# Cross-attention and expert layer: the rotation's two products moved to GpSimd, its bias to ScalarE

## Chip, cores and metric

One core of one Trainium2 chip. The metric is the device time of one execution in microseconds, the median of the runs.

## What is computed

Two layers in a row on x of shape (64, 64, 256): 64 batches, 64 channels, 256 positions. The change lies in the first, cross-attention with 8 heads of 8 channels, in the rotation of q and k. The second, sixteen experts of which each row uses two, and a shared one, comes after it in program order and is untouched.

```python
x = x + xattn(layernorm(x), ctx, ...)
x = x + ffn(layernorm(x), ...)

q = split_heads(_proj(x, Wq, bq));  k = split_heads(_proj(c, Wk, bk))
def _apply_rotary(pos, t):
    half = t.shape[-1] // 2
    rot = jnp.concatenate([-t[..., half:], t[..., :half]], axis=-1)
    return t * jnp.cos(pos) + rot * jnp.sin(pos)
scores = jnp.einsum('bhtc,bhsc->bhts', q, k) / math.sqrt(K_CH)
p_attn = jax.nn.softmax(scores, axis=-1)
```

## The kernel before

The kernel is five written-out instruction streams, one for each engine (`tensor`, `vector`, `scalar`, `gpsimd`, `sync`), that meet only at semaphores. Each stream walks the same `steps` from r = -8 to 72, and inside a step over eight places k = 0 to 7, one for each head. A step handles several batches at different stages at once (`at.has(off)` asks whether batch r + off exists): scores for the maxima of batch r + 2, transposed scores, exponentials and values of batch r, normalisation of batch r - 1, and, at offset 6, the projection and rotation of one operand of a pair of batches: q in even steps, k in odd ones. The order inside each stream is written by hand and no engine skips ahead.

The rotation, step by step (line numbers of the profile):

- TensorE, k = 4: the projection L1420 into `bank_b` (into `bank_a` at r = -5). The channels are ordered so that the two halves of the rotation lie in partitions 0 to 63 and 64 to 127.
- ScalarE, `swap`, L792: at k = 4 and k = 5, each ahead of that k's Exp (L826), one half of the bank is copied to the other half of the partitions, into `turned`.
- VectorE, k = 5, behind the reciprocal L1190 and the product L1197: L1213 makes `rc` = (bank + bias) x cos, L1215 makes `rs` = (turned + bias) x sin, both 128x256 f32, and counts `s_rope`. For r = -6 and -5 VectorE also does the rest (`split`, L972 to L980).
- GpSimd from r = -4: `qk` = rc + rs (L739), its first bf16 part (L742), the rest after it (L744); then `split_maxima` (L703, L706); then the second and third part (L750, L754). SyncE writes the parts to DRAM (L433) and reads them back as the stacked operands `QK` three steps ahead of their use (L440).

`split_maxima` splits the maxima M of batch r + 2, that VectorE's eight reductions L1157 of the step have made, into two bf16 values, Mb. TensorE transposes Mb at k = 2 of the next step (L1462), ahead of that step's L1376 (values of the second half of the heads), and of its projection L1420 at k = 4. ScalarE copies the transpose out (Mt, L860) and SyncE sends it into Q (L555).

`bank_b` is used in turn by the projection, the transposes of the normalised output (L1485, even steps, k = 6), the output projection (L1446), the transposes of normalised rows (L1504, odd steps, k = 7) and the router (L1453). TensorE's `held` waits for its last reader; for L1485 and L1504 that is `s_rope`, VectorE's products.

GpSimd also has, at the head of a step, three tiny operations in even steps (L717 to L721), and in the odd steps r = 19 to 57 two scatters of rows (L693, indirect DMAs) with a memset behind them (L730), in every second of these with an iota ahead (L681). SyncE waits for the memset before it sends Mt. From r = 58 on there is no rotation.

The functions that the change touches:

## Time and profile before

| what | value |
|---|---|
| median of 3 runs | 749.25 us (746.85 to 752.11) |
| span of the profiled execution (no other time of it is recorded) | 758.6 us |
| busy: TensorE, VectorE, ScalarE, GpSimd | 92%, 79%, 68%, 56% |

A page of the profile gives the busy share of each engine, the span in 40 slices, the chain of work that ended last, and the costliest groups of instructions. The trace behind it gives single instructions: start, length, engine, line, what is written from what, and in brackets the idle time of the engine just before and what ended it ("issue" when nothing in the profile does). PE is TensorE, DVE VectorE, ACT ScalarE, POOL GpSimd, SP SyncE; PEclk is the clock granted to TensorE as a share of 2.4 GHz.

### The profile page before, as it was taken

The page shows a single profiled execution, that of the slowest core. Times are in us where ns is not written, and L with a number is a line of the kernel's source. Part 1 is how long each engine was busy: PE and PEld are TensorE (multiplying, and loading weights), DVE is VectorE, ACT ScalarE, POOL GpSimd, SP SyncE. Part 2 cuts the span into 40 slices and gives each one's busy share as a digit, 9 for nine tenths or more (in the row PEclk, how much of TensorE's full clock was granted, in tenths as well). Part 3 has the DMA queues.
Part 4 walks back from the last instruction along what each step waited for, and adds up shares of the span by engine and source line. Part 5 has one row for each costly group of instructions (what it writes and reads, how often), then busy time and mean ns, then how long its engine had stood idle before and what let it go on. Part 6 is the DMA issues. An engine that isn't in the chain of part 4 may idle for free.

```text
span 758.6 us, 19342 instructions
## 1 busy us (share of the span) xinstructions
PE 697.3 (92%) x5941; PEld 482.6 (64%) x5941; DVE 598.5 (79%) x1597; ACT 512.7 (68%) x1211; POOL 426.0 (56%) x755
## 2 busy tenths in 40 slices
PE   2698999999999999999999999999897999999995
PEld 1355565666666666666666666666565978888784
DVE  6888999899899889989998998998645544466666
ACT  4267787888888888888888888887751155554441
POOL 3554656645756667666666566664344025655562
PEclk9999999999999999999999999999999999999998
DMA  5665543444465455544444444444073535678774
GB/s 170 175 174 161 156 124 107 124 134 145 141 176 156 150 164 147 155 131 138 142 143 152 146 121 149 137 140 153 32 225 116 165 92 162 221 244 279 230 236 151
DMA packets 97147, 118.81 MB, mean 157 GB/s; under 512 B 12821, under 2 KB 81304, under 8 KB 97049
## 3 DMA queue, kind: packets, MB, share of 16 engines
q1 hardware_dynamic: 89684, 100.16, 44.0%
q0 software_dynamic: 6864, 16.93, 6.4%
q8 instruction: 53, 0.87, 0.5%
q10 hardware_dynamic: 500, 0.49, 0.3%
q14 instruction: 46, 0.37, 0.2%
HBM read 76.87 MB, written 42.11 MB: 157 GB/s over the span
## 4 chain that ended last, share of the span: by engine, by line
PE 69%; DVE 12%; POOL 8%; issue 7%; DMA 2%; ACT 1%; another core or an unknown queue 0%; SPq 0%; ACTq 0%; DVEq 0%; POOLq 0%
PE bank_o L1376 13%; PE bank_s L1402 11%; PE bank_st L1439 10%; PE bank_st L1559 9%; DVE M L1157 5%; PE bank_s L1577 4%; PE bank_st L1354 4%; PE bank_b L1420 2%; POOL work L739 2%; POOL parts_sb L742 2%; POOL work L744 2%; PE bank_b L1446 2%; PE bank_a L1494 2%; PE bank_b L1485 2%; PE bank_s L1361 2%
## 5 line engine op out<-in xcount | busy, mean ns | idle before, releaser
L1157 DVE TENSOR_REDUCE M<-bank_s 128x2 f32<-128x512 f32 x512 | 339.3, 682 | 49.4 <-PE bank_s L1402 41.5
L826 ACT ACTIVATE Pr<-bank_st 128x512 f32<-128x512 f32 x503 | 292.6, 598 | 64.0 <-PE bank_st L1439 53.3
L1402 PE MATMUL bank_s<-QK 72*128 72x256 bf16 x1024 | 202.0, 280 | 8.8 <-DMA QK<-parts 5.9
L1439 PE MATMUL bank_st<-QK 98*128 98x256 bf16 x1006 | 195.8, 276 | 0.9 <-ACT Pr L826 0.2
L1376 PE MATMUL bank_o<-Pr,wide 128*32 128x256 f32 x2048 | 140.3, 390 | 0.5 <-ACT Pr L826 0.5
L1402 PEld LDWEIGHTS bank_s<-QK 72*128 72x128 bf16 x1024 | 91.0, 99 | 68.8 <-DVE M L1157 30.6
L739 POOL TENSOR_TENSOR work<-work 128x256 f32<-128x256 f32 x62 | 45.0, 725 | 158.5 <-DVE work L1215 158.5
L766 POOL DMA_INDIRECT results<-Pr,ids_out x79 | 78.5, 994 | 80.4 <-issue 45.7
L1439 PEld LDWEIGHTS bank_st<-QK 98*128 98x128 bf16 x1006 | 90.4, 98 | 45.9 <-ACT Pr L826 18.7
L1559 PE MATMUL bank_st<-QK,xn 128*128 x316 | 82.3, 383 | 1.0 <-issue 1.0
L1376 PEld LDWEIGHTS bank_o<-Pr,wide 128*32 128x32 f32 x2048 | 56.3, 110 | 36.0 <-issue 15.0
L693 POOL DMA_INDIRECT slots<-ring,slot x64 | 63.8, 996 | 26.2 <-issue 11.5
L1254 DVE TENSOR_TENSOR OT<-work,bank_st 128x128 f32<-128x128 f32 x79 | 22.7, 288 | 56.9 <-ACT work L917 50.7
L792 ACT ACTIVATE turned<-bank_b 64x256 f32<-64x256 f32 x126 | 47.6, 378 | 19.0 <-PE bank_b L1420 10.4
L1559 PEld LDWEIGHTS bank_st<-QK,xn 128*128 128x128 f32 x316 | 54.0, 190 | 6.7 <-issue 2.2
L1577 PE MATMUL bank_s<-wd,work 128*128 x158 | 47.4, 383 | 0.2 <-DVE Pr L1272 0.2
L742 POOL TENSOR_TENSOR parts_sb<-work 128x256 bf16<-128x256 f32 x62 | 44.9, 724 | 0.0
L754 POOL TENSOR_TENSOR parts_sb<-work,parts_sb 128x256 bf16<-128x256 f32 x62 | 41.7, 673 | 4.9
L865 ACT ACTIVATE O<-bank_o 128x256 f32<-128x256 f32 x64 | 24.5, 383 | 29.4 <-PE bank_o L1376 29.4
L744 POOL TENSOR_TENSOR work<-work,parts_sb 128x256 f32<-128x256 f32 x62 | 41.5, 669 | 4.9
L750 POOL TENSOR_TENSOR parts_sb<-work,parts_sb 128x256 bf16<-128x256 f32 x62 | 41.7, 672 | 0.0
L917 ACT ACTIVATE work<-bank_st 128x128 f32<-128x128 f32 x79 | 21.9, 277 | 27.4 <-PE bank_st L1559 26.3
(175 smaller groups left out, 1061.2 us busy)
## 6 DMA issues: line engine op xcount, KB each, us to landing
QK<-parts SPq DMA_DIRECT2D x127, 288.0 KB
parts<-parts_sb SPq DMA_DIRECT2D x64, 192.0 KB, 2.4
wide<-slots SPq DMA_DIRECT2D x79, 130.0 KB
ctx_kv<-ctx_dram SPq DMA_DIRECT2D x64, 128.0 KB, 2.4
xT_all<-results SPq DMA_DIRECT2D x14, 512.0 KB
QK<-w_gu SPq DMA_DIRECT2D x8, 512.0 KB
parts<-parts_sb SPq DMA_DIRECT2D x31, 128.0 KB, 2.9
X<-x_dram SPq DMA_DIRECT2D x7, 512.0 KB, 5.4
```

Source lines behind the costliest of these rows:

```text
L693: pool.indirect_dma_start(out=slots, out_offset=bass.IndirectOffsetOnAxis(ap=slot[:, k, n:n + 1], axis=0), in_=ring[:, row, :], in_offset= ...
L739: nc.gpsimd.tensor_tensor(qk[:, h], rc[:, h], rs[:, h], ALU.add).then_inc(s_qk, 1)
L742: nc.gpsimd.tensor_tensor(parts[:, p, h, 0, :], rc[:, h], rs[:, h], ALU.add).then_inc(s_p1, 1)
L744: nc.gpsimd.tensor_tensor(rest[:, h], qk[:, h], parts[:, p, h, 0, :], ALU.subtract).then_inc(s_r1, 1)
L766: pool.indirect_dma_start(out=results, out_offset=bass.IndirectOffsetOnAxis(ap=ids_out[:, at.mod(8, -4):at.mod(8, -4) + 1], axis=0), in_=y ...
L826: nc.scalar.activation(Pr[k][:], bank_of_scores(at.r, k)[:], ACT.Exp, scale=SCALE).then_inc(s_exp, 1)
L1157: nc.vector.tensor_reduce(M[:, c, 2 * ORDER[k]:2 * ORDER[k] + 2], bank_s[S_BANK[c][k]][:].rearrange("p (a s) -> p a s", a=2), AX.X, ALU.ma ...
L1376: last = nc.tensor.matmul(bank_o[32 * j:32 * j + 32, 0:T], Vcols[at.odd_pair(off)][:, first:first + 32], Pr[4 * group + j][:, T * chunk:T ...
L1402: last = nc.tensor.matmul(bank_s[S_BANK[at.mod(2)][k]][:, T * t:T * t + T], Q[c][0:KR, ORDER[k], P * t:P * t + P], K[c][0:KR, ORDER[k], :] ...
L1439: last = nc.tensor.matmul(bank_of_scores(at.r, k)[:, T * s:T * s + T], K[c][0:MROW + 2, ORDER[k], P * s:P * s + P], Q[c][0:MROW + 2, ORDER ...
L1559: last = nc.tensor.matmul(up_bank[m][:, 0:2 * I], xTs[m][:, c, :], weights(c), start=(c == 0), stop=(c == 1))
L1577: nc.tensor.matmul(down_bank[m][:, 0:T], aT[m][:, 0:P], weights, start=True, stop=True).then_inc(s_d, 1)
```

## The change

ScalarE adds the biases. Both turned copies become Identity activations with the bias as a pointer (a column of `bias_qk`), and behind the second stands a new one, straight, of the whole bank into a new tile `flat`, counted by a new semaphore `s_flat`. GpSimd makes both products from SBUF: `rs` from `turned` as soon as both copies are there, counted by a new `s_rs`, `rc` from `flat`, counted by `s_rope`. VectorE keeps products only for r = -6 and -5. The readers of `bank_b` that wait for the rotation now wait for `s_flat`. At r = -6 ScalarE waits for the bias before its first copy, since the bias now enters there.

```diff
@@ gpsimd, step
                     p, h = at.odd_pair(6), at.mod(2)
+                    wait(pool, s_turn, at.value(2, 14))
+                    wait(pool, s_p1, at.value(1, 5))
+                    nc.gpsimd.tensor_tensor(rs[:, h], turned[:], tab[:, 1, :], ALU.mult).then_inc(s_rs, 1)
+                    wait(pool, s_flat, at.value(1, 7))
+                    nc.gpsimd.tensor_tensor(rc[:, h], flat[:], tab[:, 0, :], ALU.mult).then_inc(s_rope, 1)
                     wait(pool, s_rope, at.value(1, 7))
+                    wait(pool, s_rs, at.value(1, 7))
@@ scalar, swap
-                wait(act, s_rope, at.value(1, 6))
-                nc.scalar.activation(turned[C * half:C * half + C], bank[C - C * half:P - C * half, 0:T],
-                                     ACT.Copy).then_inc(s_turn, 1)
+                wait(act, s_rs, at.value(1, 6))
+                if at.r == -6:
+                    act.wait_ge(s_bias, 2)
+                own = slice(C * half, C * half + C)
+                h = at.mod(2)
+                nc.scalar.activation(turned[own], bank[C - C * half:P - C * half, 0:T], ACT.Identity,
+                                     bias=bias_qk[own, 2 * h + 1:2 * h + 2]).then_inc(s_turn, 1)
+                if half:
+                    wait(act, s_rope, at.value(1, 6))
+                    nc.scalar.activation(flat[:], bank[:, 0:T], ACT.Identity,
+                                         bias=bias_qk[:, 2 * h:2 * h + 1]).then_inc(s_flat, 1)
@@ vector, step, k == 5
-                        wait(dve, s_turn, at.value(2, 14))
-                        wait(dve, s_p1, at.value(1, 5))
...
-                        bank = bank_a if at.r == -5 else bank_b
-                        nc.vector.scalar_tensor_tensor(rc[:, h, :], bank[:, 0:T], bias_qk[:, 2 * h:2 * h + 1],
-                                                       tab[:, 0, :], ALU.add, ALU.mult)
-                        nc.vector.scalar_tensor_tensor(rs[:, h, :], turned[:], bias_qk[:, 2 * h + 1:2 * h + 2],
-                                                       tab[:, 1, :], ALU.add, ALU.mult).then_inc(s_rope, 1)
+                        if at.r < -4:
+                            wait(dve, s_turn, at.value(2, 14))
+                            wait(dve, s_flat, at.value(1, 7))
+                            nc.vector.tensor_tensor(rc[:, h, :], flat[:], tab[:, 0, :], ALU.mult).then_inc(s_rope, 1)
+                            nc.vector.tensor_tensor(rs[:, h, :], turned[:], tab[:, 1, :], ALU.mult).then_inc(s_rs, 1)
@@ tensor, readers of bank_b (and the two held() calls ahead of L1485 and L1504)
-                return ((s_rope, at.value(1, 6), NB), (s_BTe, at.pairs(last, add=1), NP),
+                return ((s_flat, at.value(1, 6), NB), (s_BTe, at.pairs(last, add=1), NP),
```

How the change moves instructions. GpSimd, a step with an iota and scatters in the steady part, before (`work` is the tile that holds rc, rs, qk and rest):

```order
L681 IOTA ring 128x4
L693 DMA slots<-ring,slot 67712x260 x2
L730 MEMSET stored 1x1
L739 TENSOR_TENSOR work<-work 128x256
L742 TENSOR_TENSOR parts_sb<-work 128x256
L744 TENSOR_TENSOR work<-work,parts_sb 128x256
L703 TENSOR_TENSOR Mb<-M,newton 128x16
L706 TENSOR_TENSOR Mb<-M,Mb 128x16
L750 TENSOR_TENSOR parts_sb<-work,parts_sb 128x256
L754 TENSOR_TENSOR parts_sb<-work,parts_sb 128x256
```

and the same place after:

```order
L684 IOTA ring 128x4
L696 DMA slots<-ring,slot 67712x260 x2
L733 MEMSET stored 1x1
L741 TENSOR_TENSOR work<-turned,tab 128x256
L743 TENSOR_TENSOR work<-flat,tab 128x256
L748 TENSOR_TENSOR work<-work 128x256
L751 TENSOR_TENSOR parts_sb<-work 128x256
L753 TENSOR_TENSOR work<-work,parts_sb 128x256
L706 TENSOR_TENSOR Mb<-M,newton 128x16
L709 TENSOR_TENSOR Mb<-M,Mb 128x16
L759 TENSOR_TENSOR parts_sb<-work,parts_sb 128x256
L763 TENSOR_TENSOR parts_sb<-work,parts_sb 128x256
```

Two instructions of 128x256 now stand between the memset and the sum, and so ahead of the split of the maxima. ScalarE, the rotation of an even step before (`Pr` are the Exps):

```order
L865 ACTIVATE O<-bank_o 128x256
L826 ACTIVATE Pr<-bank_st 128x512
L792 ACTIVATE turned<-bank_b 64x256
L826 ACTIVATE Pr<-bank_st 128x512
L792 ACTIVATE turned<-bank_b 64x256
L826 ACTIVATE Pr<-bank_st 128x512 x2
L847 ACTIVATE ring<-X,vv 128x256
```

and after:

```order
L882 ACTIVATE O<-bank_o 128x256
L843 ACTIVATE Pr<-bank_st 128x512
L805 ACTIVATE turned<-bank_b,bias_qk 64x256
L843 ACTIVATE Pr<-bank_st 128x512
L805 ACTIVATE turned<-bank_b,bias_qk 64x256
L809 ACTIVATE flat<-bank_b,bias_qk 128x256
L843 ACTIVATE Pr<-bank_st 128x512 x2
L864 ACTIVATE ring<-X,vv 128x256
```

The turned copies keep their places; the straight one stands behind the second, ahead of that step's last three Exps.

## Rows read from the trace of the kernel before

**Rows 1.** The page: busy time, share of the span, instructions.

```profile
PE 697.3 (92%) x5941; PEld 482.6 (64%) x5941; DVE 598.5 (79%) x1597; ACT 512.7 (68%) x1211; POOL 426.0 (56%) x755
```

**Rows 2.** The page: the chain that ended last, by line.

```profile
PE bank_o L1376 13%; PE bank_s L1402 11%; PE bank_st L1439 10%; PE bank_st L1559 9%; DVE M L1157 5%; PE bank_s L1577 4%; PE bank_st L1354 4%; PE bank_b L1420 2%; POOL work L739 2%; POOL parts_sb L742 2%; POOL work L744 2%; PE bank_b L1446 2%; PE bank_a L1494 2%; PE bank_b L1485 2%; PE bank_s L1361 2%
```

**Rows 3.** Stretches: length, busy us by engine, clock, DMA share, GB/s.

```profile
76.18:134.82 58.64, 54.98 (x534) 35.12 (x534) 53.88 (x139) 46.52 (x102) 36.16 (x74) 1.00 0.42 126
134.82:511.88 377.06, 365.91 (x3597) 239.22 (x3596) 341.94 (x803) 312.72 (x682) 242.55 (x473) 1.00 0.48 145
```

**Rows 4.** Timeline, one even step: start, length, engine, line, operation, [idle before].

```profile
303.21 0.23 PE L1462 MATMUL bank_a<-ident_b,Mb 128*32 128x128 bf16 x1 [0.19 <-POOL Mb L706]
...
304.90 0.60 PE L1420 MATMUL bank_b<-xn,w_qk 128*128 128x256 f32 x2
...
305.54 0.38 ACT L792 ACTIVATE turned<-bank_b 64x256 f32<-64x256 f32 x1
...
305.94 0.60 ACT L826 ACTIVATE Pr<-bank_st 128x512 f32<-128x512 f32 x1
...
306.56 0.38 ACT L792 ACTIVATE turned<-bank_b 64x256 f32<-64x256 f32 x1
...
307.69 0.48 DVE L1215 SCALAR_TENSOR_TENSOR work<-turned,bias_qk,tab 128x256 f32<-128x256 f32 x1
...
308.24 0.73 POOL L739 TENSOR_TENSOR work<-work 128x256 f32<-128x256 f32 x1 [2.65 <-DVE work L1215]
308.27 0.41 PE L1485 MATMUL bank_b<-ident,On 128*128 128x128 f32 x2 [0.28 <-issue]
...
308.93 0.73 POOL L742 TENSOR_TENSOR parts_sb<-work 128x256 bf16<-128x256 f32 x1
...
309.74 0.67 POOL L744 TENSOR_TENSOR work<-work,parts_sb 128x256 f32<-128x256 f32 x1
...
310.66 0.22 POOL L706 TENSOR_TENSOR Mb<-M,Mb 128x16 bf16<-128x16 f32 x1
...
311.27 0.23 PE L1462 MATMUL bank_a<-ident_b,Mb 128*32 128x128 bf16 x1
```

**Rows 5.** Timeline, the odd steps r = 31 (first row) and r = 33.

```profile
300.52 0.72 POOL L739 TENSOR_TENSOR work<-work 128x256 f32<-128x256 f32 x1 [1.53 <-DVE work L1215]
...
314.63 0.38 ACT L792 ACTIVATE turned<-bank_b 64x256 f32<-64x256 f32 x1
...
314.74 0.09 POOL L730 MEMSET stored<- 1x1 f32 x1
...
316.57 0.72 POOL L739 TENSOR_TENSOR work<-work 128x256 f32<-128x256 f32 x1 [1.74 <-DVE work L1215]
```

**Rows 6.** Groups by line: count, busy us, mean ns of one, idle before, releasers.

```profile
L826 ACT ACTIVATE Pr<-bank_st 128x512 f32<-128x512 f32 x503 | 292.6, 598 | 64.0 <-PE bank_st L1439 53.3
...
L792 ACT ACTIVATE turned<-bank_b 64x256 f32<-64x256 f32 x126 | 47.6, 378 | 19.0 <-PE bank_b L1420 10.4 <-DVE parts_sb L980 3.9
...
L739 POOL TENSOR_TENSOR work<-work 128x256 f32<-128x256 f32 x62 | 45.0, 725 | 158.5 <-DVE work L1215 158.5
...
L865 ACT ACTIVATE O<-bank_o 128x256 f32<-128x256 f32 x64 | 24.5, 383 | 29.4 <-PE bank_o L1376 29.4
...
L837 ACT ACTIVATE xn<-X,shift,rstd 128x256 f32<-128x256 f32 x32 | 19.4, 607 | 0.9 <-DVE shift L953 0.8
...
L853 ACT ACTIVATE ring<-ring 128x512 f32<-128x512 f32 x2 | 1.3, 626 | 0.1
```

**Rows 7.** Timeline, GpSimd and VectorE at the same time.

```profile
303.11 0.67 POOL L750 TENSOR_TENSOR parts_sb<-work,parts_sb 128x256 bf16<-128x256 f32 x1
...
303.20 0.62 DVE L1050 TENSOR_TENSOR CU<-CU,route_sb 128x16 f32<-128x16 f32 x1
...
309.54 0.17 DVE L1050 TENSOR_TENSOR CU<-CU,route_sb 128x16 f32<-128x16 f32 x1
```

**Rows 8.** The chain in order of time, at the start: start, us, what.

```profile
26.45 6.02 DMA parts<-parts_sb
```

More of the change, by code:

```diff
@@ L144, in xattn_moe @@
         turned = sb("turned", [P, T])
+        flat = sb("flat", [P, T])
         beff = sb("beff", [P, 1])
@@ L277, in xattn_moe @@
         s_turn = sem("s_turn")
+        s_rs = sem("s_rs")
+        s_flat = sem("s_flat")
         s_qk = sem("s_qk")
@@ L971, in split @@
                 dve.wait_ge(s_rope, h + 1)
+                dve.wait_ge(s_rs, h + 1)
                 nc.vector.tensor_tensor(qk[:, h], rc[:, h], rs[:, h], ALU.add).then_inc(s_qk, 1)
@@ L1384, in step @@
                 if at.r == -3:
-                    pe.wait_ge(s_rope, 1)
+                    pe.wait_ge(s_flat, 1)
                     nc.tensor.matmul(bank_o[:, 0:1], w[:, 5, :], bias[:, 5:6], start=True, stop=True).then_inc(s_bo, 1)
                 if at.r == -2:
-                    pe.wait_ge(s_rope, 2)
+                    pe.wait_ge(s_flat, 2)
                 if at.r == -1:
@@ L1480, in step @@
                         wait(pe, s_On, at.value(1, 0))
-                        held(at, bank_b, (s_rope, at.value(1, 7), NB))
+                        held(at, bank_b, (s_flat, at.value(1, 7), NB))
                         if at.i is None:
@@ L1499, in step @@
                         wait(pe, s_xs, at.pairs(-5, add=1))
-                        held(at, bank_b, (s_rope, at.value(1, 7), NB))
+                        held(at, bank_b, (s_flat, at.value(1, 7), NB))
                         if at.i is None:
```

## The prediction

> A measurement of this kernel can tell about 1% (7.5 us) from no change; "step" below is one pass r of the main loop, from one transpose of the maxima (L1462 on TensorE) to the next.
>
> **What bounds the kernel now.** I read the busy shares first. TensorE shows 92% and VectorE 79%, GpSimd only 56% [rows 1]. That invites the reading "free VectorE, use GpSimd". The chain of waits corrects it: under TensorE's own lines stand VectorE's reduction L1157 and GpSimd's L739, L742 and L744 [rows 2]. GpSimd is idle for almost half of the time and is on the path all the same.
>
> Next, the stretches. From 134.82 to 511.88 us the clock granted to TensorE is 1.00 (its 2.4 GHz level) and TensorE is busy 365.91 of 377.06 us. Both ends are starts of L1462 and 47 steps lie between, so a step is 8.02 us. The seven steps before (58.64 us) take 8.38 us each, and there VectorE is busy 53.88 us, 92% [rows 3].
>
> Then one step in order of time, the thing to learn here [rows 4]. It starts with L1462 at 303.21, which had waited 0.19 us for GpSimd's Mb. The projection L1420 goes out at 304.90. ScalarE copies the first half turned, 305.54 to 305.92, does one Exp, and copies the second half, 306.56 to 306.94. VectorE's second product ends at 308.17, GpSimd starts its sum L739 at 308.24, goes on with L742 and L744, and only then splits the maxima; L706 ends at 310.88. The next L1462 needs that Mb; it starts at 311.27. The next projection stands behind it in TensorE's order. So there is a ring, TensorE - ScalarE - VectorE - GpSimd - TensorE, that closes once a step. In this even step Mb was 0.39 us early and TensorE was late, for a reason in the same rows: the transpose L1485 into bank b could go only at 308.27, just behind VectorE's products of that bank. In the odd step before it Mb was the late one. Ring and TensorE's own work are nearly equal; what the change does to the ring decides.
>
> **The change, part by part.**
>
> *VectorE loses two instructions a step.* They take 0.47 us each; the second runs from 307.69 to 308.17 [rows 4]. In the ring they are replaced, so nothing is gained there twice. Elsewhere VectorE has room: 341.94 of 377.06 us busy, so I cost this at nothing in the 47 steps; the ring hides it. In the seven early steps at 92% it is worth something: they fall from 8.38 to the ring's new 8.16, -0.22 x 7 = -1.5 us.
>
> *The turned copies get a bias pointer.* ScalarE: a copy from PSUM of 256 elements takes 383 ns and an Exp of 512 takes 598, so an element costs 0.84 ns. A Copy from SBUF of 512 takes 626, so of 256 about 411. The Identity from SBUF of 256, with a pointer for scale and one for bias, takes 607: 196 more, 98 for each pointer [rows 6]. The turned copy of 378 then takes about 0.47. Bounds: 0.38 (the pointer costs nothing) to 0.61 (that Identity's whole time); I take one pointer. Two such copies and one Exp in a row: the second copy ends 0.19 later.
>
> *The straight copy.* 383 + 98 = 0.48 us, behind the second turned copy. It ends at 306.94 + 0.19 + 0.02 + 0.48 = 307.63, before GpSimd wants it (307.89, below). It delays ScalarE's next Exps by 0.67 us together with the rest, but its Exps wait for scores for 53.3 us in the trace, 0.8 us for each of 64 steps [rows 6], and it catches up there. Cost nothing; without that cover up to 0.67 us a step. It also frees bank b at 307.63 instead of 308.17: L1485, which waited 0.28, need not wait. By TensorE's own work an even step would then take 8.06 - 0.28 + 0.09 (scores behind a later Exp) = 7.87 us; an odd one, 2 x 8.02 - 8.06 = 7.98 now, less the 0.19 that L1462 waited, 7.79, and a little less for its own use of bank b: 7.8 on the mean.
>
> *GpSimd gets both products ahead of its sum.* Its sum of two f32 operands takes 725 ns [rows 6]; no product of this size is in the trace. Bounds: 0.67 (L744, one operand bf16) and 0.95 (twice VectorE's 0.47); I take 0.725, same engine, shape and types. Starts in a row stand 0.69 apart where nothing is waited for (308.24, 308.93) and 0.81 where the engine waits for its own result (308.93, 309.74) [rows 4]. So: second turned copy ends 307.13, first product 307.20, second 307.89, sum 308.70, and from the sum's start to Mb's end are 2.64 us as before: 311.34, L1462 at 311.38. The step becomes 311.38 - 303.21 = 8.17, say 8.16 us, odd or even, since no VectorE instruction stands in it any more. TensorE (7.8) now waits for Mb every step. 47 x (8.16 - 8.02) = +6.5 us.
>
> *Steps with scatters.* In 20 odd steps (r = 19 to 57) two indirect DMAs and a memset stand between the tail of one rotation and the head of the next. GpSimd was free at 314.83, idle for 1.74 us, and began the sum at 316.57; the second turned copy had ended at 315.01 [rows 5]. The idleness is now filled by 1.50 us of products. Counted from the step's L1462 at 311.27, GpSimd was free at +3.56. Mb, 0.39 early in the even step ahead, will be just in time, so GpSimd starts its tail 0.35 later and is free at +3.91, and the copy is ready at 3.74 + 0.19 = +3.93: just enough. Ten of the steps have an iota more (idle 1.53 instead of 1.74, as before 300.52 [rows 5]); there the products start some 0.15 late, +1.5 us. The same memset lets SyncE's queue send Mt (L555), now 0.35 to 0.56 us later; TensorE, with 8.16 - 7.8 of new room before L1462, hides most of that.
>
> *The start.* ScalarE now waits for the bias before its first copies. VectorE's first products wait for three copies there. At r = -4 and -3 GpSimd has two rotations in a row, each 1.5 us longer, and behind them goes the write of the parts whose transfer starts at 26.45 in the chain [rows 8]: some 3 us later. The first full steps wait for that data. But the transfer took 6.02 us, among others that would go on meanwhile, so I count +2.5, between 0.5 and 3.5.
>
> Sum: +6.5 + 1.5 - 1.5 + 2.5 = +9.0 us. The profile has a span of 758.6 us (no other time of that execution is recorded), 9.35 above the median of the runs; I put the difference on the median: 749.25 + 9.0 = 758.3.
>
> **A rule against it.** VectorE's L1050 took 0.17 us at 309.54, and 0.62 at 303.20, while GpSimd's L750 ran from 303.11 to 303.78 [rows 7]. The Trainium skill ("SBUF — State Buffer", Who interferes with whom) says that a VectorE instruction with two SBUF inputs and a GpSimd instruction that reads SBUF exclude each other, the later one waiting for the whole of the first. The trace agrees for VectorE as the later one. By that rule 1.45 us more of GpSimd work a step would block VectorE's routing work oftener, which has room, and could hold a product back; for this I have rival D.
>
> **The rivals.**
>
> B, no change: the pointer is read in time that is hidden and the copies stay at 0.38 us. For it: the one ACTIVATE with pointers that I could price reads SBUF, and these read PSUM. Against: both copies begin only at or after the end of what they follow (305.94 + 0.60, then 306.56), so there is nothing under which a read would hide. The ring is then 307.01 + 1.50 + 2.64 + 0.04 = 311.19, 7.98 us; 47 x -0.04 = -2, plus 2.5: 749.8.
>
> C, faster: the ring is not what decides; bank b is. With its wait gone TensorE runs at 7.8 us a step: 47 x -0.22 = -10.3, + 2.5: 741.4. It decides only if Mb is ready by then, which takes both products in under 1.1 us instead of 1.5. Against it stands the 725 ns of 62 sums. The gain of the earlier bank is real and goes into the wait for Mb.
>
> D, still slower: GpSimd cannot keep up in the scatter steps, with blocked products, scatters of 1.0 us behind it and Mt sent late. Twenty steps at 0.4 more: +8, 766. For it: only 0.02 us of room by my count. Against: the remaining wait of TensorE absorbs the Mt part.
>
> E: the copies cost 0.61 each. The ring takes 0.27 more, 8.43: +19 + 2.5, 771.
>
> **How the numbers follow.** Forecast (754 to 763 by itself) 0.53, B 0.20, C 0.06, D 0.15, E 0.06. Slower by over 1% (above 756.7): two thirds of the forecast, D and E, 0.56. Faster by over 1%: C, at 741.4 just past the bound, 0.05. Within 1%: the rest, 0.39. Leaving out C below and E above, the range is 748.5 to 767.
>
> **What would show it.** Right: L1462 starts 8.16 us apart in both kinds of step and every one waits for POOL Mb; the turned copies take 0.47, the straight one 0.48; GpSimd's products 0.725; no wait at L1485; GpSimd's idleness before its first product near 0 in scatter steps and VectorE's share below 85% between the same steps; the parts' write near 29 us. Wrong: steps of 7.98 with copies of 0.38 (B); steps below 7.9 with Mb early (C); odd steps over 8.4 from r = 19 on with GpSimd never idle (D). If TensorE still waits elsewhere (scores, bank s), my claim that ScalarE catches up has failed.

## The result, and the profile after

| | kernel before | changed kernel | ratio, 95% interval |
|---|---|---|---|
| first comparison | 750.68 us (746.85 to 752.31, 4 runs) | 760.22 us (758.41 to 761.23, 4 runs) | 1.0135 [1.0097, 1.0174] |
| second comparison (the experiment "after again") | 748.01 us (745.30 to 750.50, 11 runs) | 758.73 us (755.75 to 761.43, 6 runs) | 1.0142 [1.0114, 1.017] |

The changed kernel is slower by 1.4%, by 9.5 us in the first comparison and 10.7 in the second. The forecast was 9.0 us.

The page of the changed kernel's profile, span 758.7 us, first the busy shares, then the chain that ended last, by engine and by line. TensorE's transpose of the maxima is L1478 now (L1462 before), the projection L1436, the scores L1418, the transposed scores L1455, the turned copies L805, the straight one L809, GpSimd's products L741 and L743, its sum L748, first part L751, rest L753, split of the maxima L706 and L709.

```profile
PE 697.7 (92%) x5941; PEld 482.2 (64%) x5941; DVE 549.7 (72%) x1473; ACT 546.7 (72%) x1275; POOL 515.5 (68%) x879
```

```profile
PE 43%; POOL 33%; issue 8%; ACT 7%; DMA 2%; DVE 2%; POOLq 1%; SPq 0%; ACTq 0%; DVEq 0%
PE bank_st L1575 8%; PE bank_o L1392 8%; PE bank_s L1418 5%; POOL work L748 5%; POOL work L741 5%; POOL parts_sb L751 5%; POOL work L753 5%; POOL work L743 5%; ACT Pr L843 4%; PE bank_s L1593 4%; PE bank_st L1455 4%; PE bank_st L1370 3%; PE bank_b L1436 3%; ACT turned L805 3%; POOL slots L696 2%
```

TensorE's busy share is 92% as in [rows 1], and it tells nothing of what happened. The chain does: GpSimd's lines, 2% of the span each in [rows 2], now stand five times with 5%, and the engine has a third of the chain. VectorE was relieved of 49 us of work (598.5 to 549.7) and the kernel is slower.

The stretches that answer to [rows 3], from one start of L1478 to another: seven early steps, then the 47 steps behind them.

```profile
78.35:135.55 57.20, 54.68 (x534) 35.30 (x534) 48.48 (x124) 49.97 (x109) 45.68 (x88) 1.00 0.43 130
135.55:522.17 386.62, 370.77 (x3596) 239.47 (x3596) 305.80 (x709) 336.44 (x728) 311.24 (x567) 1.00 0.47 141
```

386.62 / 47 = 8.23 us a step, against 8.02: +9.6 us in this stretch alone. The early steps fell from 8.38 to 57.20 / 7 = 8.17, -1.4 us. The clock granted to TensorE is 1.00 in both kernels, so no part of it is a matter of clock.

One even step in order of time, as [rows 4] have it of before. It goes from 291.82 to 300.07.

```profile
291.82 0.23 PE L1478 MATMUL bank_a<-ident_b,Mb 128*32 128x128 bf16 x1 [0.23 <-POOL Mb L709]
...
293.52 0.60 PE L1436 MATMUL bank_b<-xn,w_qk 128*128 128x256 f32 x2
...
294.15 0.47 ACT L805 ACTIVATE turned<-bank_b,bias_qk 64x256 f32<-64x256 f32 x1
...
295.27 0.47 ACT L805 ACTIVATE turned<-bank_b,bias_qk 64x256 f32<-64x256 f32 x1
...
295.77 0.47 ACT L809 ACTIVATE flat<-bank_b,bias_qk 128x256 f32<-128x256 f32 x1
295.82 0.73 POOL L741 TENSOR_TENSOR work<-turned,tab 128x256 f32<-128x256 f32 x1 [1.60 <-ACT turned L805]
296.51 0.81 POOL L743 TENSOR_TENSOR work<-flat,tab 128x256 f32<-128x256 f32 x1
296.51 0.22 DVE L1052 TENSOR_TENSOR route_sb<-route_sb,m 128x64 f32<-128x64 f32 x1
...
296.63 0.44 PE L1501 MATMUL bank_b<-ident,On 128*128 128x128 f32 x2
...
297.39 0.73 POOL L748 TENSOR_TENSOR work<-work 128x256 f32<-128x256 f32 x1
...
299.80 0.22 POOL L709 TENSOR_TENSOR Mb<-M,Mb 128x16 bf16<-128x16 f32 x1
300.07 0.09 PEld L1478 LDWEIGHTS bank_a<-ident_b,Mb 128*32 128x32 bf16 x1 [0.58 <-POOL Mb L709]
300.07 0.23 PE L1478 MATMUL bank_a<-ident_b,Mb 128*32 128x128 bf16 x1 [0.29 <-POOL Mb L709]
```

The reader is to follow GpSimd's column. Once the second turned copy has ended, at 295.74, GpSimd works without a pause until 300.02, the moment at which Mb is there, and TensorE has stood still for it. TensorE's own late one of before, the transpose into bank b (L1485 before, L1501 now), went at +4.81 from the step's start instead of +5.06, as its bank comes free with the straight copy. It gained nothing by that, since the next L1478 waits for Mb. Of the 47 starts of L1478 that end these steps 41 show a wait for Mb, of the load of its weights or of itself (17 before). At the other six, r = 18, 26, ..., 58, TensorE was idle for 0.11 us at most. The list of waits for the stretch has 18.0 us for the loads of weights, in 42 waits (it counts the start at r = 11 too), against 5.0 in 17 before.

Groups by line, the columns as in [rows 6]:

```profile
L805 ACT ACTIVATE turned<-bank_b,bias_qk 64x256 f32<-64x256 f32 x126 | 59.1, 469 | 20.9 <-PE bank_b L1436 10.4 <-DVE parts_sb L998 3.0 <-DVE bias_qk L1226 2.6
...
L743 POOL TENSOR_TENSOR work<-flat,tab 128x256 f32<-128x256 f32 x62 | 45.6, 736 | 0.0
L741 POOL TENSOR_TENSOR work<-turned,tab 128x256 f32<-128x256 f32 x62 | 45.5, 734 | 76.8 <-ACT turned L805 76.0
L748 POOL TENSOR_TENSOR work<-work 128x256 f32<-128x256 f32 x62 | 45.0, 726 | 4.9
...
L809 ACT ACTIVATE flat<-bank_b,bias_qk 128x256 f32<-128x256 f32 x63 | 29.9, 474 | 1.6
```

Last, a step with an iota and two scatters, of GpSimd, SyncE's queue and TensorE. It begins at 300.07 and ends with the last row.

```profile
303.15 0.98 POOL L696 DMA_INDIRECT slots<-ring,slot  x1 [0.30 <-issue]
...
304.12 0.09 POOL L733 MEMSET stored<- 1x1 f32 x1
304.18 0.74 POOL L741 TENSOR_TENSOR work<-turned,tab 128x256 f32<-128x256 f32 x1
304.24 0.68 SPq L558 DMA_DIRECT2D QK<-Mt  x1
...
306.24 0.11 PEld L1455 LDWEIGHTS bank_st<-QK 98*128 98x128 bf16 x2 [0.40 <-DMA QK<-Mt]
...
308.35 0.09 PEld L1478 LDWEIGHTS bank_a<-ident_b,Mb 128*32 128x32 bf16 x1 [0.21 <-POOL Mb L709]
```

GpSimd has no idle time ahead of its first product, which starts at +4.11 instead of +3.99: the scatters hold it. The step takes 8.28. SyncE's load of the scaled maxima, L558, goes only behind the memset, and TensorE waits 0.40 us for it; that wait is hidden here, since L1478 waits again behind it.

### The profile page after: what moved, and what is told of

It reads as the page before. It is cut to its first block, busy times and chain, and to the rows that moved or that the text cites. A ratio compares the mean times of both kernels' runs of the same rounds, so it can differ in the third digit from the quotient of the medians.

```text
span 758.7 us, 19412 instructions
## 1 busy us (share of the span) xinstructions
PE 697.7 (92%) x5941; PEld 482.2 (64%) x5941; DVE 549.7 (72%) x1473; ACT 546.7 (72%) x1275; POOL 515.5 (68%) x879
## 4 chain that ended last, share of the span: by engine, by line
PE 43%; POOL 33%; issue 8%; ACT 7%; DMA 2%; DVE 2%; POOLq 1%; SPq 0%; ACTq 0%; DVEq 0%
PE bank_st L1575 8%; PE bank_o L1392 8%; PE bank_s L1418 5%; POOL work L748 5%; POOL work L741 5%; POOL parts_sb L751 5%; POOL work L753 5%; POOL work L743 5%; ACT Pr L843 4%; PE bank_s L1593 4%; PE bank_st L1455 4%; PE bank_st L1370 3%; PE bank_b L1436 3%; ACT turned L805 3%; POOL slots L696 2%
## 5 line engine op out<-in xcount | busy, mean ns | idle before, releaser
L1418 PE MATMUL bank_s<-QK 72*128 72x256 bf16 x1024 | 201.6, 280 | 8.1 <-DMA QK<-parts 7.3
L1455 PE MATMUL bank_st<-QK 98*128 98x256 bf16 x1006 | 195.7, 276 | 7.6 <-DMA QK<-Mt 1.3
L1418 PEld LDWEIGHTS bank_s<-QK 72*128 72x128 bf16 x1024 | 93.2, 99 | 63.7 <-issue 38.9
L1455 PEld LDWEIGHTS bank_st<-QK 98*128 98x128 bf16 x1006 | 88.7, 98 | 57.2 <-ACT Pr L843 31.7
L741 POOL TENSOR_TENSOR work<-turned,tab 128x256 f32<-128x256 f32 x62 | 45.5, 734 | 76.8 <-ACT turned L805 76.0
L805 ACT ACTIVATE turned<-bank_b,bias_qk 64x256 f32<-64x256 f32 x126 | 59.1, 469 | 20.9 <-PE bank_b L1436 10.4
L748 POOL TENSOR_TENSOR work<-work 128x256 f32<-128x256 f32 x62 | 45.0, 726 | 4.9
L743 POOL TENSOR_TENSOR work<-flat,tab 128x256 f32<-128x256 f32 x62 | 45.6, 736 | 0.0
L753 POOL TENSOR_TENSOR work<-work,parts_sb 128x256 f32<-128x256 f32 x62 | 42.1, 679 | 4.9
L751 POOL TENSOR_TENSOR parts_sb<-work 128x256 bf16<-128x256 f32 x62 | 45.0, 726 | 0.0
L763 POOL TENSOR_TENSOR parts_sb<-work,parts_sb 128x256 bf16<-128x256 f32 x62 | 41.6, 670 | 4.9
```

The source lines that it names most:

```text
L741: nc.gpsimd.tensor_tensor(rs[:, h], turned[:], tab[:, 1, :], ALU.mult).then_inc(s_rs, 1)
L743: nc.gpsimd.tensor_tensor(rc[:, h], flat[:], tab[:, 0, :], ALU.mult).then_inc(s_rope, 1)
L748: nc.gpsimd.tensor_tensor(qk[:, h], rc[:, h], rs[:, h], ALU.add).then_inc(s_qk, 1)
L751: nc.gpsimd.tensor_tensor(parts[:, p, h, 0, :], rc[:, h], rs[:, h], ALU.add).then_inc(s_p1, 1)
L753: nc.gpsimd.tensor_tensor(rest[:, h], qk[:, h], parts[:, p, h, 0, :], ALU.subtract).then_inc(s_r1, 1)
L805: nc.scalar.activation(turned[own], bank[C - C * half:P - C * half, 0:T], ACT.Identity, bias=bias_qk[own, 2 * h + 1:2 * h + 2]).then_inc(s ...
```

## The experiments

Step times below are of the same 47 steps: the time from L1478 (or its like) at r = 11 to the one at r = 58, divided by 47. By kind they are means over the even steps, the odd ones r = 13, 17, ... ("odd, a") and the odd ones r = 11, 15, ... ("odd, b", with an iota from r = 19 on). Ratios are to the kernel before in the same comparison. It took 760.66 us in the one of no bias and the two spare sums, 763.41 in the next four, 748.01 in the last three: its level differs from chip to chip by 2%, so only ratios of one comparison are compared, and steps.

| kernel | ratio to before, 95% | step us | even | odd, a | odd, b |
|---|---|---|---|---|---|
| before | 1 | 8.02 | 8.06 | 8.00 | 7.98 |
| changed kernel | 1.0135 [1.0097, 1.0174] | 8.23 | 8.23 | 8.17 | 8.28 |
| the same again | 1.0142 [1.0114, 1.017] | 8.22 | 8.23 | 8.17 | 8.27 |
| changed, no bias | 1.0002 [0.9981, 1.0022] | 8.07 | 7.99 | 8.05 | 8.25 |
| before, spare sum in the ring | 1.0323 [1.0302, 1.0344] | 8.52 | 8.50 | 8.55 | 8.54 |
| before, spare sum outside it | 1.0066 [1.0041, 1.009] | 8.11 | 8.07 | 8.06 | 8.25 |
| before, split early | 0.9893 [0.9855, 0.9931] | 7.92 | 8.07 | 7.85 | 7.72 |
| changed, split early | 0.9925 [0.9894, 0.9955] | 8.02 | 7.89 | 8.05 | 8.22 |
| changed, products on VectorE | 0.9891 [0.9852, 0.9931] | 7.93 | 7.89 | 8.03 | 7.91 |
| changed, products on VectorE, split early | 0.9823 [0.9786, 0.986] | 7.90 | 7.89 | 7.99 | 7.83 |
| changed, split early, load free | 0.9849 [0.9824, 0.9874] | 7.88 | 7.89 | 7.93 | 7.81 |
| changed, products on VectorE, split early, load free | 0.9819 [0.9794, 0.9843] | 7.87 | 7.89 | 7.94 | 7.78 |

In the row of the spare sum in the ring, three even steps of 9.8 to 9.9 us are counted in; without them the even ones are 8.28 to 8.31. They are looked at with that experiment.

**The kernel before once more**, unchanged, one profiled execution.

> The kernel before, unchanged, for a second profile. The first one has a span of 758.6 us while the runs of that kernel have a median of 750.7, and 246.7 us of it lie behind the last rotation, where the changed kernel needs 236.5. If the difference belongs to that one execution, the 47 steps take 377 us again (8.02 each) and the part behind the last rotation is 8 to 10 us shorter, near 237. If it belongs to the kernel, it is 246 again, and the change would have gained 10 us behind the rotations and lost 20 ahead of them.

Its 47 steps took 8.02 us each, as in the profile ahead of the prediction: the steps are a steady measure. What lies ahead of them is not: L1462 of r = 0 came at 42.73 us here and at 40.58 in the first profile, and the seven early steps took 8.56 us each instead of 8.38. The part behind the last step took 246.5 us, as in that profile too (246.7), while in the changed kernel's profile it had been 236.5. That question is taken up at the end of this section.

**No bias on ScalarE.** The biases of q and k are left out.

```diff
-                nc.scalar.activation(turned[own], bank[C - C * half:P - C * half, 0:T], ACT.Identity,
-                                     bias=bias_qk[own, 2 * h + 1:2 * h + 2]).then_inc(s_turn, 1)
+                nc.scalar.activation(turned[own], bank[C - C * half:P - C * half, 0:T],
+                                     ACT.Copy).then_inc(s_turn, 1)
...
-                    nc.scalar.activation(flat[:], bank[:, 0:T], ACT.Identity,
-                                         bias=bias_qk[:, 2 * h:2 * h + 1]).then_inc(s_flat, 1)
+                    nc.scalar.activation(flat[:], bank[:, 0:T], ACT.Copy).then_inc(s_flat, 1)
```

> The changed kernel with its three copies as plain Copy without the bias pointer; the bias of q and k is left out. Ring theory: the two turned copies take 0.38 again instead of 0.47, the second ends 0.19 us earlier, and since the step is set by the ring, the step falls from 8.23 to 8.04 us on the mean (8.17 to 7.98 without routing): 47 x 0.19 = 9 us less than the changed kernel, about 751, ratio to before 1.00. Rival (GpSimd's load or its conflicts with VectorE set the step): ScalarE is no bound at 72%, nothing changes by more than 2 us, about 758 to 760, ratio 1.01.

The group of the turned copies by line:

```profile
L805 ACT ACTIVATE turned<-bank_b 64x256 f32<-64x256 f32 x126 | 47.6, 378 | 21.2 <-PE bank_b L1435 11.5 <-DVE parts_sb L997 3.3 <-DVE bias_qk L1225 2.0
```

378 ns instead of 469: the pointer costs 91 ns here, on data from PSUM, and the two copies of a step cost 0.18 us of the ring. The Trainium skill ("ScalarE: Activation LUTs", What ACT_TABLE_LOAD costs) gives about 93 ns for each such operand; the runs agree. The steps fell by 0.15 of the 0.20 us that the change had added, and the kernel is level with the one before, with the same two products still on GpSimd. The ten iota steps did not fall, 8.30 on the mean in both kernels: GpSimd's first product starts there directly behind the memset, at +4.09 to +4.11 without the bias and at +4.10 to +4.12 with it, however early the copies are (at r = 19 at +4.28 in both).

**A spare sum in the ring.** In the kernel before, GpSimd adds two halves of the table into a tile that nobody reads, between the first part and the rest, ahead of the split.

```diff
                     nc.gpsimd.tensor_tensor(parts[:, p, h, 0, :], rc[:, h], rs[:, h], ALU.add).then_inc(s_p1, 1)
+                    nc.gpsimd.tensor_tensor(spare[:], tab[:, 0, :], tab[:, 1, :], ALU.add)
                     wait(pool, s_p1, at.value(1, 7))
```

> The kernel before with one spare sum of 128x256 on GpSimd in each rotation, in the ring: ahead of the rest L744, so ahead of the split of the maxima. Ring theory: Mb comes 0.7 us later. Odd steps go from 7.98 to 8.67, even ones, in which Mb had 0.39 - 0.04 us of room, from 8.06 to 8.40: +0.51 us on the mean of 47 steps, +24 us, ratio 1.032. Load theory: the same as the next kernel, whatever it is.

**The same spare sum outside the ring**, a few lines on, behind the split.

```diff
                                             ALU.subtract).then_inc(s_p2, 1)
+                    nc.gpsimd.tensor_tensor(spare[:], tab[:, 0, :], tab[:, 1, :], ALU.add)
                     wait(pool, s_p2, at.value(1, 7))
```

> The kernel before with the same spare sum, but behind the split of the maxima. The same work, the same engine, the same step. Ring theory: GpSimd's idleness of 1.5 to 2.7 us before its next rotation takes it, no change within 0.3% (Mt in the scatter steps goes 0.7 later and may cost up to 3 us in all). Load theory (GpSimd's share or its conflicts with VectorE cost the time): slower by 1% or more, as the change was, which added two such instructions.

Both theories' numbers for the sum outside were missed: 1.0066 lies over the 0.3% of the ring and under the 1% of the load. Groups by line, first of the sum inside, then of the sum outside:

```profile
L744 POOL TENSOR_TENSOR spare<-tab 128x256 f32<-128x256 f32 x62 | 45.3, 730 | 0.0
```

```profile
L753 POOL TENSOR_TENSOR spare<-tab 128x256 f32<-128x256 f32 x62 | 45.3, 730 | 0.0
```

The same 730 ns of the same engine, 62 times, cost 3.2% in the one place and 0.7% in the other. It is not GpSimd's load that counts but the place in its queue. Inside, the odd steps grew by 0.56 us and the plain even ones by 0.22, where 0.69 and 0.34 were expected. Both are 0.12 to 0.13 short: GpSimd's starts stand 0.81 apart where it waits for its own first part and 0.69 otherwise [rows 4], and the sum fills that wait, so it costs 0.57 and not 0.7. The step table shows a mean of +0.50 all the same, since in three even steps of the profiled execution (r = 28, 44, 56) the clock fell. The stretches of r = 26 and r = 28, columns as in [rows 3]:

```profile
263.01:271.29 8.28, 7.85 (x77) 5.26 (x77) 6.71 (x14) 6.76 (x16) 5.32 (x12) 1.00 0.38 106
279.82:289.67 9.85, 9.41 (x78) 5.97 (x78) 6.54 (x14) 6.83 (x16) 5.33 (x12) 0.83 0.51 157
```

In the second TensorE ran in part at its lower level, 1.2 GHz: 0.83 over 9.85 us is 1.7 us of full clock lost, and the step is 1.57 us longer. In the one ahead TensorE had been busy for 7.85 of 8.28 us at full clock. What made it fall in these three and in no other stays open. Without the three the mean is 8.42, +0.40 a step, 19 us of the 25 by which the medians differ. The other executions had mean clocks of 0.986 to 0.993, like those of the kernel before, and took 783 to 786 us, so the ratio is not a matter of clock; but that it came out at the expected 1.032 is in part luck. Where the other 6 us lie these profiles do not show. Outside, even and plain odd steps stayed within 0.07 us of before, and the odd ones of kind b grew from 7.98 to 8.25: 12 x 0.27 = 3.2 us of the 4.2 that the 47 steps lost. The list of waits over the 47 steps of this kernel names what holds them (what waits, for whom: us, times, longest):

```profile
PEld bank_st L1441 <- DMA QK<-Mt: 10.4, 19, 0.9
```

and in the kernel before:

```profile
PEld bank_st L1439 <- DMA QK<-Mt: 0.8, 4, 0.3
```

So there is a second path beside the ring: GpSimd's tail, its scatters, its memset, SyncE's wait for it, the load of the scaled maxima, TensorE's transposed scores.

**The split of the maxima ahead of the rest**, once in the kernel before and once in the changed one. The split then fills the gap in which GpSimd waits for its own first part.

```diff
                     nc.gpsimd.tensor_tensor(parts[:, p, h, 0, :], rc[:, h], rs[:, h], ALU.add).then_inc(s_p1, 1)
+                    if at.has(2) and at.r != -2:
+                        split_maxima(at)
                     wait(pool, s_p1, at.value(1, 7))
...
-                if at.has(2) and at.r != -2:
+                if at.has(2) and at.r != -2 and not at.has(6):
                     split_maxima(at)
```

> The kernel before with the split of the maxima one instruction earlier on GpSimd: behind the first part (L742) instead of behind the rest (L744). Ring theory: Mb comes about 0.7 us earlier, the ring is open and TensorE's own work sets the step: odd steps 7.98 - 0.19 = 7.79, even ones stay at 8.06, since there L1485 waits for VectorE's products (bank b). Mean 7.93: 47 x -0.1 = -4.5 us, ratio 0.994. If Mb is not what odd steps wait for: no change.

> The changed kernel with the split one instruction earlier in the same way. Ring theory: Mb at about +7.4 us instead of +8.12, the ring no longer sets the step, and now the earlier release of bank b by ScalarE's straight copy counts: 7.8 to 7.9 us a step, odd and even, 47 x -0.35 = -16 us against the changed kernel, -7 against before: about 743, ratio 0.99. Steps with scatters may be longer, since GpSimd has then some 8 us of work in a step of 7.8 to 7.9. Rival (GpSimd is overloaded or conflicts with VectorE): GpSimd's work is the same, so it stays near 758 to 760.

In the kernel before, the forecast of the steps (7.93) was met with 7.92, all of it in the odd steps. The ratio was not: 0.9893, 9 us, where 0.994 was expected. The 47 steps give 4.7 of these; in the profile r = 11 begins at 130.6 us, where the two profiles of the kernel before have 134.8 and 136.6, so about as much was won ahead of the 47 steps. The even ones stayed at 8.06 to 8.07. The timeline of one shows why:

```profile
296.63 0.23 PE L1464 MATMUL bank_a<-ident_b,Mb 128*32 128x128 bf16 x1
...
301.11 0.47 DVE L1217 SCALAR_TENSOR_TENSOR work<-turned,bias_qk,tab 128x256 f32<-128x256 f32 x1
...
301.68 0.41 PE L1487 MATMUL bank_b<-ident,On 128*128 128x128 f32 x2 [0.28 <-issue]
...
304.69 0.23 PE L1464 MATMUL bank_a<-ident_b,Mb 128*32 128x128 bf16 x1
```

L1487 still goes at +5.05, just behind VectorE's product of bank b. An even step of the changed kernel with the early split:

```profile
296.35 0.23 PE L1480 MATMUL bank_a<-ident_b,Mb 128*32 128x128 bf16 x1
...
300.29 0.47 ACT L811 ACTIVATE flat<-bank_b,bias_qk 128x256 f32<-128x256 f32 x1
...
301.15 0.44 PE L1503 MATMUL bank_b<-ident,On 128*128 128x128 f32 x2
...
304.23 0.23 PE L1480 MATMUL bank_a<-ident_b,Mb 128*32 128x128 bf16 x1
```

L1503 goes at +4.80 and the step is 7.88. That is the gain hidden in the change: ScalarE's straight copy frees the bank earlier, 0.18 us an even step, and it shows once the ring is shorter.

The ratio is near the 0.99 expected, but the forecast of the steps was missed: 8.02 where 7.8 to 7.9 was expected. The odd steps were 8.05 and 8.22. One of them:

```profile
292.27 0.09 POOL L733 MEMSET stored<- 1x1 f32 x1
...
292.39 0.68 SPq L558 DMA_DIRECT2D QK<-Mt  x1
...
294.43 0.11 PEld L1457 LDWEIGHTS bank_st<-QK 98*128 98x128 bf16 x2 [0.57 <-DMA QK<-Mt]
```

TensorE waits for the load of the second path, 8.5 us in 15 of the 47 steps, where I had looked at the ring alone.

**The products back on VectorE**, with ScalarE's three copies kept: once as the only edit to the changed kernel, once together with the early split.

```diff
@@ gpsimd
-                    wait(pool, s_turn, at.value(2, 14))
-                    wait(pool, s_p1, at.value(1, 5))
-                    nc.gpsimd.tensor_tensor(rs[:, h], turned[:], tab[:, 1, :], ALU.mult).then_inc(s_rs, 1)
-                    wait(pool, s_flat, at.value(1, 7))
-                    nc.gpsimd.tensor_tensor(rc[:, h], flat[:], tab[:, 0, :], ALU.mult).then_inc(s_rope, 1)
@@ vector
-                        if at.r < -4:
...
+                        wait(dve, s_turn, at.value(2, 14))
+                        wait(dve, s_p1, at.value(1, 5))
+                        nc.vector.tensor_tensor(rs[:, h, :], turned[:], tab[:, 1, :], ALU.mult).then_inc(s_rs, 1)
+                        wait(dve, s_flat, at.value(1, 7))
+                        nc.vector.tensor_tensor(rc[:, h, :], flat[:], tab[:, 0, :], ALU.mult).then_inc(s_rope, 1)
```

> The changed kernel with both products back on VectorE, which makes them from SBUF as in the changed kernel's first two steps (turned x sine, then straight x cosine); ScalarE's three copies with bias and the release of bank b stay. Ring theory: two products on VectorE behind its On cost about 0.8 us instead of 1.5 on GpSimd; Mb at about +7.6 in even and +7.9 in odd steps; bank b free early: steps of 7.9, 47 x -0.12 = -5 us against before, but the start keeps part of its delay and the early steps at 8.38 stay bound by VectorE: 746 to 749, ratio 0.995 to 1.0. If ScalarE's added 0.67 us a step were the cost of the change, it would be as slow as the changed kernel, 1.013.

> The last one and the early split together. Ring theory: the ring is open in every step, TensorE sets 7.8 to 7.87 us: about -2 us against the kernel without the early split, and GpSimd has none of its load. Against the changed kernel with the early split it tells whether GpSimd's products cost anything outside the ring: if that one is slower by 3 us or more, its scatter steps or conflicts with VectorE do.

This parts the change in two. The copies alone make the kernel faster: 0.9891, steps 8.02 to 7.93. The steps are as expected (7.9); the ratio is better than the 0.995 to 1.0 expected, and the start kept none of its delay (r = 11 begins at 133.5 us in the profile, against 134.8 and 136.6 in those of the kernel before). Moving the products costs 8.23 - 7.93 = 0.30 us a step, 14 us in the 47 steps. VectorE's groups by line, of the kernel with both edits:

```profile
L1229 DVE TENSOR_TENSOR work<-flat,tab 128x256 f32<-128x256 f32 x64 | 27.3, 426 | 0.3
L1227 DVE TENSOR_TENSOR work<-turned,tab 128x256 f32<-128x256 f32 x64 | 26.6, 416 | 3.8 <-ACT turned L802 3.5
```

416 and 426 ns against 734 and 736 on GpSimd, 0.63 us a step for the pair. The steps show only half of it: the even ones are down at 7.89, a level that every kernel with the straight copy and a shorter ring shares and that I read as TensorE's own work. And VectorE, the engine that the change relieved, does it at no visible price: with the early split this is a kernel that beats both, 0.9823. Against the changed kernel with the early split it is 8.4 us faster, past the 3 us from which, by the expectation, the products cost something outside the ring too; the next two runs look for it.

**Without SyncE's wait for the memset**, on top of the early split; and all three edits together. Load and scatters share no data; the wait only orders them.

```diff
-                    if at.r in STORES and at.r < DRAIN:
-                        sp.wait_ge(s_stored, held_by_stores(at.r))
                     alone(s_tme, at.value(1, 2))
```

> The changed kernel with the split of the maxima ahead of the waiting sums, as in the run of that alone, and without SyncE's wait for the scatter store ahead of the load of the scaled maxima. The theory that the loads' way (memset, SyncE's wait, load, TensorE's scores) is the second path of the steps with a scatter expects the steps that took 8.32 with it to fall to the level of the other odd ones, 8.07 or under: 23 steps by 0.25 us or 5 to 6 us less than with the early split alone, a ratio to the kernel before of 0.985. The rival, that GpSimd itself is late there (the memset and the scatter stand in its own queue ahead of the next sums), expects the steps to stay at 8.3 and the ratio at 0.992.

> VectorE makes both products, ScalarE all copies, the split comes early, and SyncE does not wait for the scatter store ahead of the load. With it the scatter steps took 7.84 us, under the plain odd ones (8.00), so by the theory that the ring of copy, products and sums decides there is nothing to gain from the load: steps as without this edit, 7.90, ratio 0.982. If the load's way were what holds these steps, they would fall below 7.8 and the ratio to 0.978 or less.

The step of kind b with the products on GpSimd:

```profile
286.36 0.23 PE L1478 MATMUL bank_a<-ident_b,Mb 128*32 128x128 bf16 x1
...
287.24 0.68 SPq L556 DMA_DIRECT2D QK<-Mt  x1
...
290.63 0.09 POOL L731 MEMSET stored<- 1x1 f32 x1
...
294.21 0.09 PEld L1478 LDWEIGHTS bank_a<-ident_b,Mb 128*32 128x32 bf16 x1
```

The load goes 0.88 us after the transpose instead of 4.26, no wait of TensorE's for it is left among the 47 steps, and kind b fell from 8.22 to 7.81, under the 8.07 that was the most the theory allowed. GpSimd's memset and first product stand as late as before in the step, so the rival, that GpSimd is late by itself, fell. The ratio is the expected one, 0.985, and the steps are level with those of the kernel with the products on VectorE, 7.88 and 7.87. With the products on VectorE the wait had cost next to nothing: steps 7.90 and 7.87, ratios 0.9823 and 0.9819, also as expected. Both of these kernels beat the kernel before by 1.8%.

**The changed kernel once more**, unchanged.

> The changed kernel once more, unchanged. Each theory expects the 47 steps behind the first twelve to take 8.23 us each as before, since the chain from TensorE's transpose over the copies, the sums and the split is its own. What differs is the part behind the last step: in the first profile of the changed kernel it took 236.5 us, in that of the kernel before and of every kernel since 246 to 254 us. If the short part belongs to the changed kernel's own code, it is there again and the ratio to the kernel before comes out at 1.000 to 1.014, however long the kernel before takes here. If it belonged to that one execution, the part takes 246 us or more here, and the ratio is what the steps and the start say: 47 times 0.204 us = 9.6, with 1 to 2 us from the start and the early steps taken together, 1.012 to 1.016 over some 760.

The steps are 8.22 us again, and the early ones 8.17. The part behind r = 58 is 234.5 us in its profile, and 234.4 in those of both other kernels of this comparison, on the same chip, where the kernel before took 748.01 us. In the profiles taken where the kernel before took 760 us or more, it is 246 to 254 us whatever the kernel. So the short part belongs to the chip or the execution and not to the changed kernel; the ratio stands at 1.014 and the reading by steps holds.

## Why the prediction was right

- *The ring decides.* Right. Forecast was 8.16 us for a plain step, TensorE waiting for Mb; measured are 8.17, and 8.17 in every early step too. That it is the place in the ring and not GpSimd's load was shown by the two spare sums. The price of the place was shown as well by the early split, which takes no work away and 0.21 us off the changed kernel's step.
- *The pointer.* 98 ns forecast, 91 measured, copies of 0.47 (forecast 0.47 and 0.48). Rival B (pointer free) and E (0.61) fall. B's ring was right by itself: without the operands the even steps are 7.99 (B's ring: 7.98), the mean with the scatter steps 8.07, and the kernel is level with the one before.
- *The products on GpSimd.* 0.725 forecast, 0.734 and 0.736 measured, starts 0.69 apart. The sum starts at +5.49 in a step without contention, as forecast.
- *Steps with an iota.* +0.15 forecast, +0.11 measured. Plain scatter steps had "just enough" room: 8.17.
- *The Mt part of rival D.* "TensorE hides most of that": right for this kernel, and only for it. The wait is there (0.40 us) and is hidden by the longer ring; as soon as the ring was shortened it came out and cost the experiment with the early split its forecast. Rival D as a whole, 0.4 us a step, fell.
- *Early steps.* -1.5 forecast; 57.20 us against 58.64, -1.4. The second profiles have 57.2 against 59.9, -2.8: the changed kernel's early steps are steady at 8.17, those of the kernel before are not.
- *The start.* +2.5 forecast. The first two profiles have +2.1 (L1478 of r = 0 at 42.72 instead of 40.58), the second two nothing (42.60 and 42.73). The parts' write did go 3 us later, at 29.08 instead of 26.03, as forecast; that the first full steps pay for it is not shown, since one kernel's start moves by as much from one execution to another.
- *ScalarE catches up.* The prediction named further waits of TensorE as the sign that this claim had failed, and part of that sign is there: in the 47 steps the weight loads of the transposed scores wait for Exps for 24.5 us in 71 waits (L1455), against 13.8 in 49 before (L1439). In the changed kernel the wait for Mb covers it. With the ring shortened it shows: the six steps r = 17, 25, ..., 57 take 8.09 us, as against 7.99 in the kernel before.
- *Rival C.* The earlier bank is real (L1501 0.25 us earlier, even steps of 7.89 where I had worked out 7.87) and went into the wait for Mb, as said. The mean of TensorE's own work was put too low: 7.8 against 7.87 to 7.88 in the two kernels with nothing left to wait for. Most odd steps do take 7.76 there (forecast 7.79 or a little less), but the six with r = 17, 25, ..., 57 take 8.09. Before, TensorE did not wait for Mb in these, and the prediction took the 0.19 off every odd step.
- *Mis-sized:* the even steps. The sum had no term for VectorE holding back GpSimd. Even steps took up to 8.26, 0.06 us over the plain ones on the mean, 23 x 0.06 = +1.3 us. In the step shown above, GpSimd's product L743 took 0.81 instead of 0.73 where VectorE's L1052, 0.22 long, began with it at 296.51. In the even step ahead of it the same befell the rest L753 (0.75 instead of 0.67), with VectorE's L1055 beginning 0.01 us behind it. In the five even steps without such a routing instruction there (r = 18, 26, ..., 50) GpSimd's instructions keep their length and the step is 8.17. The kernel without bias is the test: its copies are earlier, so GpSimd's product begins 0.19 us ahead of VectorE's instruction, and now VectorE's is the long one.

```profile
289.25 0.73 POOL L743 TENSOR_TENSOR work<-flat,tab 128x256 f32<-128x256 f32 x1
289.44 0.62 DVE L1051 TENSOR_TENSOR route_sb<-route_sb,m 128x64 f32<-128x64 f32 x1
```

Its even steps are all alike, 7.98 to 8.01. So it is the coincidence of the two starts that lengthens GpSimd's instruction. The rule of the Trainium skill ("SBUF — State Buffer", Who interferes with whom) lets the one that comes later wait for the whole of the other. In direction the trace agrees. In size it does not: GpSimd lost 0.08 us and not VectorE's 0.22, and in [rows 7] VectorE lost 0.45 (0.62 instead of 0.17) where 0.58 of GpSimd's instruction was left.

The terms: 47 steps +9.6 (forecast +6.5 and +1.5), early steps -1.4 (-1.5), start +2.1 (+2.5), together +10.3; 9.5 and 10.7 were measured. Of these only the first is the same in both pairs of profiles (+9.6 and +9.5). At r = 11 the kernel before stands at 134.8 and 136.6 us, the changed one at 135.6 and 133.6, so the terms ahead of it come to anything from +0.7 to -3.0 by the profiles. The mechanism in the steps is right; that the total came within 2 us of the forecast is in part luck, since the steps cost 1.6 us more than forecast and the start and the early steps cannot be told to that precision.

## What to carry to other kernels

Where engines hand one item round in a ring once a step, price an edit by what it puts between the two ends of the ring, and not by busy shares: 0.73 us of GpSimd cost 3.2% in the ring and 0.7% behind it, and an engine busy 56% was the one that set the time. Look then for what a ring carries without need: moving two tiny instructions (the split) ahead of a wait gave 1.1% in the kernel before (half of it in the 47 steps), keeping the copies and leaving the products on the faster engine gave the same, both together 1.8%. And before forecasting a shorter ring, look for the next path, here a memset, a wait of SyncE's and a load, which the longer ring had covered.

## What the runs showed beside this

The part behind r = 58 differs by 12 us between profiles of the same part of the program. Its windows of the kernel before, of the changed kernel, and of the changed kernel in the second comparison:

```profile
511.88:758.60 246.72, 224.59 (x1479) 178.27 (x1478) 142.83 (x515) 113.33 (x349) 110.70 (x138) 0.98 0.56 178
```

```profile
522.17:758.70 236.53, 220.68 (x1479) 177.52 (x1478) 142.49 (x515) 113.86 (x349) 110.76 (x138) 0.98 0.59 185
```

```profile
520.09:754.60 234.51, 219.06 (x1479) 176.70 (x1478) 142.38 (x515) 113.57 (x349) 110.78 (x138) 0.99 0.59 187
```

VectorE, ScalarE and GpSimd are busy for the same time to within 0.6 us; from the first row to the third the span is 12.2 shorter, and TensorE only 5.5 less busy. At 579 us of the first profile 10.6 of the 12.2 are already there. The 47 steps ahead differ by 0.003 us a step between two executions of the changed kernel, so it is not the whole chip that is slow. The clock granted does not tell them apart: it is 0.98 in the first and in the second, which are 10.2 us apart. In the longer profiles an engine there sits idle for 2 to 4 us ahead of single instructions with no releaser that the profile shows, TensorE for 2.69 us ahead of L1453 at 574.72 in the first. What these wait for stays open. It accounts for the 9.35 us by which the profile ahead of the prediction stood over the median of its runs: that profile had the long part, and the median fits the short one.
